# Four-layer graph kernel: the last rows of layer 0 in two groups, gate weights between root and rows, x transfers moved

## The chip, the cores and the metric

The kernel runs on one core of a Trainium2 chip. Times are device microseconds of one execution. TensorE (PE) multiplies, VectorE (DVE), ScalarE (ACT) and GpSimd (POOL) work elementwise, and SyncE (SP) issues DMAs. Each engine runs its own list of instructions in order; they meet at semaphores.

## The reference

There are 4096 nodes with 64 features and a sparse 0/1 matrix adj of 4096 x 4096. Four graph layers follow one another, each with a residual and a layer norm. Cut to what matters:

```python
# layer 0: the last 100 neighbours of each row, weights halved with each step back
rank = cumsum(mask, axis=1); deg = rank[:, -1:]
w = mask * where(pos > 0, 0.5 ** (k - pos), 0)
x = layernorm(x + w @ (x @ W0) + b0)
# layer 1: two gated steps (GRU), each over the whole matrix
m = adj @ (x @ W); gi = m @ wih.T + bih; gh = x @ whh.T + bhh
r, z = sigmoid(...), sigmoid(...); n = tanh(i_n + r * h_n)
h = relu((1 - z) * n + z * x)          # and once more with other weights
x = layernorm(x + h2)
# layers 2 and 3: a normalized product, a mean over neighbours
x = layernorm(x + (dinv * (adj + I) * dinv) @ x @ W2)
x = layernorm(x + concat([x, adj @ x / (deg + 1)]) @ W3.T)
```

## The kernel before, in words

The program numbers its five passes over the matrix 0 to 4: pass 0 is the first layer (called layer 0 in the code and here), 1 and 2 are the gated steps, 3 and 4 the last two layers. The matrix stays in SBUF as fp8 (adjT). Nodes come in 32 tiles of 128 (index jb), or 8 groups g of 512. A pass computes for each group g the product of all 32 tiles of the rows S (a high and a low f16 piece of the scaled x, 128 columns together) with 512 columns of adjT: product(layer, g, first, last), L1083, issues the matmuls of tiles first to last. combine(layer, g), L911, applies the small weights to the finished group.

Layer 0 goes in four quarters q of 1024 nodes (Q = 4, B = 4 tiles in a group). Each quarter ends in rows0 (L562) and norm (L516) on VectorE: sums, means, squares and variances, each as two instructions (both_halves, L499), then a wait for GpSimd. There root (L302) raises the variances to the power -1/2; it waits for var_ready and signals rstd_ready. Then VectorE writes the normalized rows xrow, and split_rows0 (L581) makes of them the two pieces of S[1] and adds 2 to s_ready, one for each group. For the last quarter that is L807, L808 and the last root, L337.

The products of the gated pass on tiles 0 to 23 are placed in layer 0, in slots on TensorE (BETWEEN, L1026), and at the head of layer1 (L1132). What needs tiles 24 to 31 waits for the last quarter: product waits for s_ready to reach 8 + jb / 4 + 1. Between them stand gate_sums (L1109), which multiplies weight pairs in PSUM and turns the degrees, and open_gates (L1122), which waits for the four signals of gate_const and for the degrees (deg_step), and clears the gate banks. Behind open_gates ScalarE writes the biases (seed, L422), and ScalarE and VectorE form m of the first group (take_y, hi_of_m, m_lo): the m path. combine(1, 0) waits for that and for the x transfer below.

gate_weights (L711) on VectorE forms the gates' constants: two zero fills, wx16 and part of wl16 out of the loaded weights w_h (gate_const 1), the biases (2, 3), and wm16 and the rest of wl16 out of gate_sums' result (4). degrees (L811) follows.

SP's queue: it loads biases and w_gates (L262) and the degree rows when layer 0 has ended, then transposes each group of S[1] into x16 by DMA (loop at L274). The upper half of x16 holds the loaded weights until they are used, so the fifth transpose waits for gate_const 4. x_high (L266) copies the high piece of a group beside m (mx16, three buffers, x_beside). The first three stand behind the eighth transpose. The order on each engine is the order in which the code is written; nothing reorders it.

Of the kernel before, what the change touches and what calls it, by code (L numbers as in the profile page):

```python
# [21 lines left out]
N, D = 4096, 64  # L22
P = 128
# [40 lines left out]
def build(nc, a):  # L64
    with ExitStack() as ctx:
# [182 lines left out]
        def _(sp):  # L248
# [25 lines left out]
            for layer in TURNS:  # L274
                for g in range(G):
                    sp.wait_ge(s_ready, layer * G + g + 1)
                    if layer == 1 and g == G // 2:
                        sp.wait_ge(gate_const, 4)
                    if layer > 1:
                        sp.wait_ge(combined, min(layer, 3) * G - G + g + 1)  # L280
                    sp.dma_start_transpose(x16[:, g * GC:(g + 1) * GC].rearrange("p (b r) -> p b r", b=B),  # L281
                                           S[layer % 2][:, g * B:(g + 1) * B, :].rearrange("p b d -> p (b d)"))\
                        .then_inc(xT_in[g], 16)
                    if layer == 2:
                        x_high(1 + (g + 3) // G, (g + 3) % G)
                if layer == 1:
                    sp.wait_ge(masked_ready, Q * NM * B)
                    x_high(1, 0)
                    x_high(1, 1)
                    x_high(1, 2)  # L290
                if layer == 2:
                    for g in range(3, G):
                        x_high(2, g)
# [7 lines left out]
        def _(pool):  # L301
            def root(n, blocks):  # L302

                pool.wait_ge(var_ready, n + 1)
                nc.gpsimd.tensor_tensor(rstd[:, 0:blocks], stat[:, 2, 0:blocks], mhalf[:, 0:blocks], ALU.pow)\  # L305
                    .then_inc(rstd_ready, 1)
# [30 lines left out]
            root(Q - 1, 2 * B)  # L337
# [6 lines left out]
            for layer in (2, 3, 4):  # L344
                for g, (_, nb) in enumerate(UNITS[layer]):
                    n = Q + (layer - 2) * G + g
# [140 lines left out]
        def _(dve):  # L487
# [11 lines left out]
            def both_halves(step, signal=None):  # L499


                for h in range(2):
# [3 lines left out]
                    if h == 1 and signal is not None:  # L506
                        ins.then_inc(signal, 1)
                    else:
                        did(ins)
                        last[h] = steps[0]  # L510
# [5 lines left out]
            def norm(n, z, zc, sq, dst, ready, meanwhile=None):  # L516
# [11 lines left out]
                                                              ALU.mult, ALU.add), var_ready)  # L528
# [33 lines left out]
            def rows0(q, out=True):  # L562
# [8 lines left out]
                norm(q, wide[0], wide[1], wide[2], pair if out else None, rows0_ready)  # L571
# [139 lines left out]
            def gate_weights():  # L711
# [7 lines left out]
                                               op0=ALU.mult, op1=ALU.subtract).then_inc(gate_const, 1)  # L719
                dve.wait_ge(biases_in, 16)  # L720
# [86 lines left out]
            rows0(Q - 1)  # L807
            split_rows0(Q - 1)  # L808
            gate_weights()

# [33 lines left out]
            for layer in range(1, LAYERS):  # L844
# [7 lines left out]
                for g, (b0, nb) in enumerate(UNITS[layer]):  # L852
# [49 lines left out]
                    norm(Q + (layer - 2) * G + g, z[:, 0:nb, :], zc[:, 0:nb, :], sq[:, 0:nb, :],  # L902
# [7 lines left out]
        def _(pe):  # L910
# [198 lines left out]
            def gate_sums():  # L1109
# [8 lines left out]
                pe.wait_ge(rows0_ready, Q)  # L1118
# [3 lines left out]
            def open_gates():  # L1122

                pe.wait_ge(rows0_ready, Q)
# [7 lines left out]
            def layer1():  # L1132
# [3 lines left out]
                product(1, 3, 0, 24)  # L1136
                gate_sums()
                product(1, 0, 24, 32)
                product(1, 1, 24, 31)
                open_gates()  # L1140
                product(1, 1, 31, 32)
                product(1, 2, 24, 32)
                product(1, 3, 24, 32)
                product(1, 4, 0, 9)
                combine(1, 0)
                product(1, 4, 9, 23)
                combine(1, 1)
                product(1, 4, 23, 32)
                product(1, 5, 0, 5)
                combine(1, 2)  # L1150
                product(1, 5, 5, 20)
                combine(1, 3)
                product(1, 5, 20, 32)
                product(1, 6, 0, 4)
                combine(1, 4)
                product(1, 6, 4, 20)
                combine(1, 5)
                product(1, 6, 20, 32)
# [171 lines left out]
```

## Time and profile before

| | before |
|---|---|
| median of 3 runs | 430.13 us (429.86 to 430.8) |
| profiled execution | 430.51 us |
| its span | 428.7 us |
| PE busy | 404.7 us, 94% |
| DVE / ACT / POOL busy | 295.4 / 215.1 / 116.8 us |
| mean granted clock of TensorE | 0.99 |

The span is the time between the first and last instruction of the profiled execution; the execution itself is longer by what lies around it. Matmuls overlap, so a row of products is busy for longer than the pitch of its instructions times their number by the tail of its last one. In a timeline the bracket behind a row is the idle time of that engine before it, and what ended it.

### The profile page before, as it was taken

To read this page: it belongs to the slowest core of one execution; us is meant where nothing else is said; L and a number is where in the kernel's file an instruction comes from. 1 tells how busy PE (TensorE), PEld (TensorE's weight loads), DVE (VectorE), ACT (ScalarE), POOL (GpSimd) and SP (SyncE) were. 2 spreads that over 40 slices of the span, in tenths; PEclk is the share of its full clock that TensorE was granted. 3 is DMA by queue.
4 is the path that set the end of the run, shared out by engine and by line. 5 is a ranking of instruction groups with operands and counts; after the bars stand their busy time and mean duration, and the time that the engine had idled before them with its cause. 6 is when DMAs were issued, how large, how long until landed. Compare 5 with 4: busy or idle time off the path is not lost.

```text
span 428.7 us, 6431 instructions
## 1 busy us (share of the span) xinstructions
PE 404.7 (94%) x2243; PEld 191.2 (45%) x2258; DVE 295.4 (69%) x862; ACT 215.1 (50%) x345; POOL 116.8 (27%) x154
## 2 busy tenths in 40 slices
PE   5878989999999999998999999999999999999991
PEld 2332433434344444444555555555554444445480
DVE  3377968867976787473964566776949566477773
ACT  2566788688868877506864554635222121212100
POOL 8213223231420100015231304234325434311111
PEclk9998999999999999999999999999999999999997
DMA  8999999999999994173011110000000101100000
GB/s 144 108 115 106 107 107 108 107 108 107 109 107 107 107 108 44 44 95 67 20 42 33 38 32 6 8 7 2 0 2 13 27 12 26 26 14 26 25 26 13
DMA packets 26241, 24.68 MB, mean 58 GB/s; under 512 B 14776, under 2 KB 17624, under 8 KB 26208
## 3 DMA queue, kind: packets, MB, share of 16 engines
q0 software_dynamic: 9360, 16.78, 39.1%
q1 hardware_dynamic: 16704, 7.41, 8.0%
q8 instruction: 18, 0.29, 0.3%
q10 hardware_dynamic: 144, 0.07, 0.1%
q14 instruction: 15, 0.12, 0.1%
HBM read 69.32 MB, written 1.06 MB: 164 GB/s over the span
## 4 chain that ended last, share of the span: by engine, by line
PE 80%; DMA 7%; DVE 4%; POOL 2%; issue 2%; ACT 1%; SPq 1%; POOLq 0%; DVEq 0%; ACTq 0%
PE Y L1099 45%; PE both L1008 15%; DMA adjT<-in_adjT 6%; PE both L987 3%; PE Y L987 3%; PE both L1015 3%; PE both L999 2%; PE Y L999 2%; PE both L959 2%; SPq L281 1%; PE both L955 1%; PE both L957 1%; POOL rstd L305 1%; POOL adjT L333 1%; DMA work<-x 1%
## 5 line engine op out<-in xcount | busy, mean ns | idle before, releaser
L1099 PE MATMUL Y<-adjT,S 128*128 128x512 fp8e4 (+1 forms) x1056 | 231.0, 373 | 0.8 <-DVE S L587 0.8
L1099 PEld LDWEIGHTS Y<-adjT,S 128*128 128x128 f16 x1056 | 101.8, 98 | 109.0 <-DVE S L587 0.9
L417 ACT ACTIVATE wgt<-both,consts 128x512 int16<-128x512 f32 x160 | 106.9, 687 | 33.6 <-PE both L1008 29.9
L305 POOL TENSOR_TENSOR rstd<-stat,mhalf 128x4 f32<-128x4 f32 (+2 forms) x29 | 35.1, 1212 | 149.1 <-DVE stat L527 149.1
L1008 PE MATMUL both<-adjT,tri 128*128 128x512 fp8e4 x160 | 61.3, 384 | 2.9 <-DMA adjT<-in_adjT 2.7
L1008 PE MATMUL both<-adjT,fix 128*128 128x512 fp8e4 x152 | 58.4, 384 | 2.3 <-ACT wgt L417 1.1
L333 POOL DMA_DIRECT2D adjT<-in_adjT x63 | 36.9, 593 | 78.8 <-DMA adjT<-in_adjT 78.8
L547 DVE SCALAR_TENSOR_TENSOR work<-Y,yT 64x512 f32<-64x512 f32 x30 | 20.8, 695 | 47.6 <-ACT yT L376 47.4
L376 ACT ACTIVATE yT<-Y 64x512 f32<-64x512 f32 x30 | 17.6, 587 | 65.2 <-PE Y L1099 41.6
L320 POOL TENSOR_TENSOR S<-work,S 128x256 f16<-128x256 f32 x24 | 18.8, 785 | 48.0 <-ACT S L401 27.4
L387 ACT ACTIVATE work<-work 64x512 f16<-64x512 f32 x30 | 18.8, 627 | 26.1 <-DVE work L547 24.6
L1008 PEld LDWEIGHTS both<-adjT,fix 128*128 128x128 bf16 x152 | 14.8, 97 | 37.6 <-ACT wgt L417 22.8
L987 PE MATMUL both<-wgt,S 128*128 128x512 bf16 x77 | 29.4, 381 | 0.3 <-ACT wgt L417 0.3
L987 PE MATMUL Y<-wgt,S 128*128 128x512 bf16 x72 | 27.3, 379 | 0.0
L614 DVE TENSOR_SCALAR work<-adjT 128x3072 int16<-128x3072 fp8e4 x12 | 21.1, 1756 | 7.6 <-PE both L999 7.6
L637 DVE TENSOR_TENSOR work<-work 128x1024 uint16<-128x1024 int16 x36 | 24.6, 684 | 0.9 <-ACT work L414 0.3
L626 DVE TENSOR_TENSOR work<-work 128x1024 int16<-128x1024 int16 x36 | 24.6, 682 | 0.0
L414 ACT ACTIVATE work<-both,consts 128x512 int16<-128x512 f32 x24 | 16.0, 688 | 15.8 <-PE both L1015 15.7
L433 ACT ACTIVATE both<-biases 128x1024 f32<-128x1024 f32 x16 | 16.1, 1011 | 15.0 <-PE both L1128 15.0
L553 DVE TENSOR_TENSOR work<-work 64x512 f16<-64x512 f32 x30 | 20.6, 687 | 3.6 <-ACT work L387 2.8
L1008 PEld LDWEIGHTS both<-adjT,tri 128*128 128x128 bf16 x160 | 15.7, 98 | 13.2 <-issue 5.1
L603 DVE TENSOR_TENSOR x<-adjT 128x1024 uint16<-128x1024 uint16 x12 | 8.2, 686 | 17.5 <-DMA adjT<-in_adjT 14.5
(129 smaller groups left out, 477.6 us busy)
## 6 DMA issues: line engine op xcount, KB each, us to landing
adjT<-in_adjT POOLq DMA_DIRECT2D x63, 256.0 KB, 39.0
work<-x SPq DMA_DIRECT2D x16, 64.0 KB, 2.0
out_rows<-xrow SPq DMA_DIRECT2D x7, 128.0 KB, 1.9
xrow<-in_xrow SPq DMA_DIRECT2D x1, 640.0 KB, 7.2
x<-in_w_gates SPq DMA_DIRECT2D x1, 512.0 KB, 5.8
biases<-in_biases SPq DMA_DIRECT2D x1, 384.0 KB, 4.2
x<-S SPq DMA_TRANSPOSE x24, 2.4
xrow<-in_xrow SPq DMA_DIRECT2D x1, 256.0 KB, 3.6
```

The source lines that it names most:

```text
L305: nc.gpsimd.tensor_tensor(rstd[:, 0:blocks], stat[:, 2, 0:blocks], mhalf[:, 0:blocks], ALU.pow)\
L320: nc.gpsimd.tensor_tensor(s[:, :, D:2 * D], ts[:, :, :], s[:, :, 0:D], ALU.subtract).then_inc(s_ready, 1)
L333: pool.dma_start(adjT[:, q, 2 * jp:2 * jp + 2, :], a["adjT"][q, jp]).then_inc(load[i % NLOAD], 16)
L417: nc.scalar.activation(wgt[:, c, tiles % 2, :], V[c][:, :], ACT.Relu, bias=tile_bias[sums]).then_inc(w_ready[c], 1)
L547: nc.vector.scalar_tensor_tensor(out=m[D:P, e % 2, :], in0=bank(layer, g)[D:P, :], scalar=1.0 / SCALE, in1=yT[D:P, e % 2, :], op0=ALU.mult ...
L553: nc.vector.tensor_tensor(m16[0:D, e % 2, :], m[D:P, e % 2, :], m16[D:P, e % 2, :], ALU.subtract)\
L614: nc.vector.tensor_scalar(wq[:, 1:B, :], adjT[:, q, quad * B + 1:(quad + 1) * B, :], -float(STEP), None, ALU.mult)\
L626: nc.vector.tensor_tensor(wq[:, k, :], wq[:, k, :], seen_now, ALU.bitwise_and).then_inc(masked_ready, 1)
L637: nc.vector.tensor_tensor(out.bitcast(U16), seen_now, wq[:, k, :], ALU.add).then_inc(seen_step, 1)
L987: mm = nc.tensor.matmul(own[c], S[0][:, jb, :], wgt[:, c, TILES.index(jb) % 2, :].bitcast(BF16), start=first, stop=(jb == 0), skip_group_c ...
L1008: return nc.tensor.matmul(V[c][:, :], (tri, fix)[which][:, :], adj_tile(q, at, c), start=start, stop=(which == 0 and s == NS - 1), skip_gr ...
L1099: mm = nc.tensor.matmul(bank(layer, g)[:, 0:nb * P], S[layer % 2][:, jb, :], cols[:, jb, :], start=(jb == 0), stop=(jb == JB - 1), skip_gr ...
```

## The change

The last 1024 rows are normalized by two roots of four columns in place of one of eight. In norm both halves of the variances now signal var_ready (each=True), and a new function last_rows writes xrow and S[1] for groups 6 and 7 apart, with one signal for each. Later roots and norms count one higher. gate_weights is cut in two: the part that works on w_h alone stands ahead of last_rows, and the rest (gate_products) behind it. On TensorE four products of tiles 24 to 27 stand ahead of gate_sums, open_gates comes after ten more products in place of fifteen, and one product of pass 1 goes from before combine(1, 0) to behind combine(1, 5). On SP the first three x_high stand ahead of the fifth transpose.

```diff
--- before.py
+++ after.py
@@ -275,6 +275,9 @@
                 for g in range(G):
                     sp.wait_ge(s_ready, layer * G + g + 1)
                     if layer == 1 and g == G // 2:
+                        sp.wait_ge(masked_ready, Q * NM * B)
+                        for first in range(3):
+                            x_high(1, first)
                         sp.wait_ge(gate_const, 4)
                     if layer > 1:
                         sp.wait_ge(combined, min(layer, 3) * G - G + g + 1)
@@ -283,11 +286,6 @@
                         .then_inc(xT_in[g], 16)
                     if layer == 2:
                         x_high(1 + (g + 3) // G, (g + 3) % G)
-                if layer == 1:
-                    sp.wait_ge(masked_ready, Q * NM * B)
-                    x_high(1, 0)
-                    x_high(1, 1)
-                    x_high(1, 2)
                 if layer == 2:
                     for g in range(3, G):
                         x_high(2, g)
@@ -299,10 +297,10 @@
 
         @block.gpsimd
         def _(pool):
-            def root(n, blocks):
+            def root(n, blocks, first=0):
 
                 pool.wait_ge(var_ready, n + 1)
-                nc.gpsimd.tensor_tensor(rstd[:, 0:blocks], stat[:, 2, 0:blocks], mhalf[:, 0:blocks], ALU.pow)\
+                nc.gpsimd.tensor_tensor(rstd[:, first:first + blocks], stat[:, 2, first:first + blocks], mhalf[:, 0:blocks], ALU.pow)\
                     .then_inc(rstd_ready, 1)
 
             def split_rows(layer, g):
@@ -334,7 +332,8 @@
                     if q >= 2 and n == 5:
                         root(q - 2, 2 * B)
             root(Q - 2, 2 * B)
-            root(Q - 1, 2 * B)
+            root(Q - 1, B)
+            root(Q, B, B)
 
             pool.wait_ge(deg_step, 1)
             nc.gpsimd.tensor_tensor(dinv[:, :], deg1[:, :], mhalf[:, :], ALU.pow).then_inc(dinv_pow, 1)
@@ -343,7 +342,7 @@
             pool.wait_ge(dinv_ready, 2)
             for layer in (2, 3, 4):
                 for g, (_, nb) in enumerate(UNITS[layer]):
-                    n = Q + (layer - 2) * G + g
+                    n = Q + 1 + (layer - 2) * G + g
                     root(n, nb)
                     if layer == 2 and g < G - 1:
 
@@ -496,14 +495,14 @@
 
                 dve.wait_ge(chain, steps[0])
 
-            def both_halves(step, signal=None):
+            def both_halves(step, signal=None, each=False):
 
 
                 for h in range(2):
                     if last[h] > 0:
                         dve.wait_ge(chain, last[h])
                     ins = step(h)
-                    if h == 1 and signal is not None:
+                    if (h == 1 or each) and signal is not None:
                         ins.then_inc(signal, 1)
                     else:
                         did(ins)
@@ -513,7 +512,7 @@
 
                 return [slice(h * blocks // 2, (h + 1) * blocks // 2) for h in range(2)]
 
-            def norm(n, z, zc, sq, dst, ready, meanwhile=None):
+            def norm(n, z, zc, sq, dst, ready, meanwhile=None, each=False):
 
 
                 H = halves(z.shape[1])
@@ -525,7 +524,7 @@
                 both_halves(lambda h: nc.vector.tensor_tensor(sq[:, H[h], :], zc[:, H[h], :], zc[:, H[h], :], ALU.mult))
                 both_halves(lambda h: nc.vector.tensor_reduce(stat[:, 1, H[h]], sq[:, H[h], :], AX, ALU.add))
                 both_halves(lambda h: nc.vector.tensor_scalar(stat[:, 2, H[h]], stat[:, 1, H[h]], 1.0 / D, EPS,
-                                                              ALU.mult, ALU.add), var_ready)
+                                                              ALU.mult, ALU.add), var_ready, each)
                 if dst is None:
                     return
                 if meanwhile is not None:
@@ -559,7 +558,7 @@
                 nc.vector.tensor_tensor(xrow[:, 2 * q * B:(2 * q + 2) * B, :], wide[1],
                                         rstd[:, :, None].to_broadcast([P, 2 * B, D]), ALU.mult).then_inc(rows0_ready, 1)
 
-            def rows0(q, out=True):
+            def rows0(q, out=True, each=False):
 
                 pair = xrow[:, 2 * q * B:(2 * q + 2) * B, :]
                 if q == 0:
@@ -568,7 +567,21 @@
                 both_halves(lambda h: nc.vector.scalar_tensor_tensor(
                     out=wide[0][:, h * B:(h + 1) * B, :], in0=gates[0][:, 2 + h, :].rearrange("p (b d) -> p b d", d=D),
                     scalar=1.0 / (Y0_SCALE * SCALE), in1=pair[:, h * B:(h + 1) * B, :], op0=ALU.mult, op1=ALU.add))
-                norm(q, wide[0], wide[1], wide[2], pair if out else None, rows0_ready)
+                norm(q, wide[0], wide[1], wide[2], pair if out else None, rows0_ready, each=each)
+
+            def last_rows():
+
+                for h in range(2):
+                    g = G - 2 + h
+                    blk, part = slice(g * B, (g + 1) * B), slice(h * B, (h + 1) * B)
+                    dve.wait_ge(rstd_ready, Q + h)
+                    nc.vector.tensor_tensor(xrow[:, blk, :], wide[1][:, part, :],
+                                            rstd[:, part, None].to_broadcast([P, B, D]), ALU.mult).then_inc(rows0_ready, 1)
+                    dve.wait_ge(rows0_ready, Q + h)
+                    did(nc.vector.tensor_scalar(S[1][:, blk, 0:D], xrow[:, blk, :], SCALE, None, ALU.mult))
+                    after()
+                    nc.vector.scalar_tensor_tensor(out=S[1][:, blk, D:2 * D], in0=xrow[:, blk, :], scalar=SCALE,
+                                                   in1=S[1][:, blk, 0:D], op0=ALU.mult, op1=ALU.subtract).then_inc(s_ready, 1)
 
             def pick_degree(q, c):
 
@@ -717,6 +730,8 @@
                 after()
                 nc.vector.scalar_tensor_tensor(out=wl16[0:D, :, 0:3 * D], in0=w_h[0:D, :, :], scalar=GATE / SCALE, in1=wx16[0:D, :, :],
                                                op0=ALU.mult, op1=ALU.subtract).then_inc(gate_const, 1)
+            def gate_products():
+
                 dve.wait_ge(biases_in, 16)
                 nc.vector.tensor_tensor(gbias[:, :, D:3 * D], gbias[:, :, D:3 * D], brz, ALU.add).then_inc(gate_const, 1)
                 dve.wait_ge(gate_const, 2)
@@ -804,9 +819,10 @@
             take_y(0, 6)
             take_y(0, 7)
 
-            rows0(Q - 1)
-            split_rows0(Q - 1)
+            rows0(Q - 1, False, True)
             gate_weights()
+            last_rows()
+            gate_products()
 
             def degrees():
 
@@ -899,7 +915,7 @@
                         both_halves(lambda h: nc.vector.tensor_tensor(z[:, H[h], :], t1[:, H[h], :], t2[:, H[h], :], ALU.add))
                     if layer == 2 and g >= 1:
                         dve.wait_ge(rows_ready, G + g)
-                    norm(Q + (layer - 2) * G + g, z[:, 0:nb, :], zc[:, 0:nb, :], sq[:, 0:nb, :],
+                    norm(Q + 1 + (layer - 2) * G + g, z[:, 0:nb, :], zc[:, 0:nb, :], sq[:, 0:nb, :],
                          None if layer == 2 and g < G - 1 else xrow[:, blk, :], rows_ready,
                          messages)
                     if layer == 4 and in_halves(4, g + 1):
@@ -1115,13 +1131,13 @@
                     mm.then_inc(gate_prod, 1)
                 pe.wait_ge(deg_in, 16)
                 pe.wait_ge(unit_ready, 1)
-                pe.wait_ge(rows0_ready, Q)
+                pe.wait_ge(rows0_ready, Q + 1)
                 nc.tensor.matmul(gates[0][:, 2, 0:JB], deg_mat[:, :], identity[0:JB, 0:JB], start=True, stop=True)\
                     .then_inc(deg_turned, 1)
 
             def open_gates():
 
-                pe.wait_ge(rows0_ready, Q)
+                pe.wait_ge(rows0_ready, Q + 1)
                 pe.wait_ge(gate_const, 4)
                 pe.wait_ge(deg_step, 1)
                 for half in range(2):
@@ -1134,28 +1150,29 @@
                 combine(0, 6)
                 combine(0, 7)
                 product(1, 3, 0, 24)
+                product(1, 0, 24, 28)
                 gate_sums()
-                product(1, 0, 24, 32)
-                product(1, 1, 24, 31)
+                product(1, 0, 28, 32)
+                product(1, 1, 24, 30)
                 open_gates()
-                product(1, 1, 31, 32)
+                product(1, 1, 30, 32)
                 product(1, 2, 24, 32)
                 product(1, 3, 24, 32)
-                product(1, 4, 0, 9)
+                product(1, 4, 0, 8)
                 combine(1, 0)
-                product(1, 4, 9, 23)
+                product(1, 4, 8, 22)
                 combine(1, 1)
-                product(1, 4, 23, 32)
-                product(1, 5, 0, 5)
+                product(1, 4, 22, 32)
+                product(1, 5, 0, 4)
...
```

VectorE between the statistics of the last quarter and the degrees; wl and wx are the gate weights, S the pieces. Before:

```order
L535 TENSOR_TENSOR xrow<-hrow,rstd 128x512 [waits rstd_ready]
L585 TENSOR_SCALAR S<-xrow 128x8x64 [waits rows0_ready]
L587 SCALAR_TENSOR_TENSOR S<-xrow,S 128x8x64 [waits chain]
L714 MEMSET wl 64x2x32 [waits gate_in]
L715 MEMSET wl 64x2x32
L716 TENSOR_SCALAR wx<-x 128x384
L718 SCALAR_TENSOR_TENSOR wl<-x,wx 64x2x192 [waits chain]
L721 TENSOR_TENSOR biases<-biases 128x2x128 [waits biases_in]
L723 TENSOR_SCALAR biases<-biases 128x512 [waits gate_const]
L726 TENSOR_SCALAR wm<-both 128x384 [waits gate_prod]
L728 SCALAR_TENSOR_TENSOR wl<-both,wm 64x2x192 [waits chain]
L814 TENSOR_SCALAR deg<-both 128x32 [waits deg_turned,gate_const]
```

and now, where gate_prod's waiter follows behind the last row shown:

```order
L727 MEMSET wl 64x2x32 [waits gate_in]
L728 MEMSET wl 64x2x32
L729 TENSOR_SCALAR wx<-x 128x384
L731 SCALAR_TENSOR_TENSOR wl<-x,wx 64x2x192 [waits chain]
L578 TENSOR_TENSOR xrow<-hrow,rstd 128x256 [waits rstd_ready]
L581 TENSOR_SCALAR S<-xrow 128x4x64 [waits rows0_ready]
L583 SCALAR_TENSOR_TENSOR S<-xrow,S 128x4x64 [waits chain]
L578 TENSOR_TENSOR xrow<-hrow,rstd 128x256 [waits rstd_ready]
L581 TENSOR_SCALAR S<-xrow 128x4x64 [waits rows0_ready]
L583 SCALAR_TENSOR_TENSOR S<-xrow,S 128x4x64 [waits chain]
L736 TENSOR_TENSOR biases<-biases 128x2x128 [waits biases_in]
L738 TENSOR_SCALAR biases<-biases 128x512 [waits gate_const]
```

Four instructions of gate_weights have moved ahead of the wait for rstd_ready, and three row instructions of 512 columns have become six of 256.

TensorE from gate_sums (the 128x192 matmuls on x) to open_gates (ones, cutw). Before:

```order
L1114 MATMUL both<-x 128x192 [waits y0_out1,gate_in]
L1114 MATMUL both<-x 128x192
L1119 MATMUL both<-unit,deg_mat 128x32 [waits rows0_ready,unit_ready,deg_in]
L1099 MATMUL Y<-adjT,S 128x512 [waits s_ready]
L1099 MATMUL Y<-adjT,S 128x512 x3
L1099 MATMUL Y<-adjT,S 128x512 [waits s_ready]
L1099 MATMUL Y<-adjT,S 128x512 x3
L1099 MATMUL Y<-adjT,S 128x512 [waits s_ready]
L1099 MATMUL Y<-adjT,S 128x512 x3
L1099 MATMUL Y<-adjT,S 128x512 [waits s_ready]
L1099 MATMUL Y<-adjT,S 128x512 x2
L1128 MATMUL both<-ones,cutw 128x512 [waits deg_step,gate_const,rows0_ready]
```

and now:

```order
L1115 MATMUL Y<-adjT,S 128x512 [waits s_ready]
L1115 MATMUL Y<-adjT,S 128x512 x3
L1130 MATMUL both<-x 128x192 [waits y0_out1,gate_in]
L1130 MATMUL both<-x 128x192
L1135 MATMUL both<-unit,deg_mat 128x32 [waits rows0_ready,unit_ready,deg_in]
L1115 MATMUL Y<-adjT,S 128x512 [waits s_ready]
L1115 MATMUL Y<-adjT,S 128x512 x3
L1115 MATMUL Y<-adjT,S 128x512 [waits s_ready]
L1115 MATMUL Y<-adjT,S 128x512 x3
L1115 MATMUL Y<-adjT,S 128x512 [waits s_ready]
L1115 MATMUL Y<-adjT,S 128x512
L1144 MATMUL both<-ones,cutw 128x512 [waits deg_step,gate_const,rows0_ready]
```

Four products with their wait for s_ready stand ahead of gate_sums, and ten in place of fifteen between it and open_gates.

SP's queue from the first transpose of the rows (x<-S) to the x transfers (work<-x). Before:

```order
L281 DMA_TRANSPOSE x<-S 128x4x128 [waits s_ready] x4
L281 DMA_TRANSPOSE x<-S 128x4x128 [waits gate_const,s_ready]
L281 DMA_TRANSPOSE x<-S 128x4x128 [waits s_ready] x3
L272 DMA work<-x 64x512 [waits xT_in0,masked_ready]
L272 DMA work<-x 64x512 [waits xT_in1]
L272 DMA work<-x 64x512 [waits xT_in2]
```

and now:

```order
L284 DMA_TRANSPOSE x<-S 128x4x128 [waits s_ready] x4
L272 DMA work<-x 64x512 [waits xT_in0,masked_ready,s_ready]
L272 DMA work<-x 64x512 [waits xT_in1]
L272 DMA work<-x 64x512 [waits xT_in2]
L284 DMA_TRANSPOSE x<-S 128x4x128 [waits gate_const]
L284 DMA_TRANSPOSE x<-S 128x4x128 [waits s_ready] x3
```

The three transfers stand ahead of the transpose that waits for gate_const.

## Rows read from the trace of the kernel before

**Rows 1.** The page's part 4, shares of the span by engine.

```profile
PE 80%; DMA 7%; DVE 4%; POOL 2%; issue 2%; ACT 1%; SPq 1%; POOLq 0%; DVEq 0%; ACTq 0%
```

**Rows 2.** The chain that ended last: start us, us, what.

```profile
186.05 1.65 POOL rstd L305
...
188.98 0.69 DVE S L587
...
192.19 0.57 DVE wl L728
...
198.04 1.98 DMA work<-x
...
231.16 6.91 PE Y L1099 x32
```

**Rows 3.** Timeline, 178 to 206 us, TensorE: start us, us, engine, line.

```profile
182.17 5.34 PE L1099 MATMUL Y<-adjT,S 128*128 128x512 fp8e4 x24
...
187.44 0.92 PE L1114 MATMUL both<-x 64*128 64x192 f32 x4
...
188.56 0.38 PE L1119 MATMUL both<-unit,deg_mat 32*128 32x32 f32 x2 [0.20 <-DVE xrow L535]
...
189.73 3.41 PE L1099 MATMUL Y<-adjT,S 128*128 128x512 fp8e4 x15 [0.79 <-DVE S L587]
...
193.56 5.77 PE L1099 MATMUL Y<-adjT,S 128*128 128x512 fp8e4 x26
...
200.27 0.24 PE L955 MATMUL both<-wx,x 128*128 128x192 f16 x1 [0.94 <-DMA work<-x]
```

**Rows 4.** Waits of TensorE from 200 us to the end: total, times, longest.

```profile
PE both L955 <- DMA work<-x: 1.4, 2, 0.9
```

**Rows 5.** Timeline, 178 to 206 us, VectorE.

```profile
185.69 0.28 DVE L527 TENSOR_SCALAR stat<-stat 128x4 f32<-128x4 f32 x2
...
189.63 0.11 DVE L714 MEMSET wl<- 64x64 uint32 x1
...
190.82 0.41 DVE L721 TENSOR_TENSOR biases<-biases 128x256 f32<-128x256 f32 x1
...
191.61 0.55 DVE L726 TENSOR_SCALAR wm<-both 128x384 f16<-128x384 f32 x1
...
192.79 0.19 DVE L814 TENSOR_SCALAR deg<-both 128x32 f32<-128x32 f32 x1
```

**Rows 6.** Timeline, VectorE, 256-column instructions, 0 to 36 us and 322 to 326 us.

```profile
29.47 0.28 DVE L669 TENSOR_SCALAR S<-xrow 128x256 f16<-128x256 f32 x1
29.78 0.43 DVE L671 SCALAR_TENSOR_TENSOR S<-xrow,S 128x256 f16<-128x256 f32 x1
...
324.73 0.43 DVE L535 TENSOR_TENSOR xrow<-work,rstd 128x256 f32<-128x256 f32 x1 [0.18 <-POOL rstd L305]
```

**Rows 7.** Timeline, VectorE and GpSimd around two later roots.

```profile
323.14 0.69 DVE L553 TENSOR_TENSOR work<-work 64x512 f16<-64x512 f32 x1
323.19 1.51 POOL L305 TENSOR_TENSOR rstd<-stat,mhalf 128x4 f32<-128x4 f32 x1 [8.26 <-DVE stat L527]
...
379.11 0.69 DVE L547 SCALAR_TENSOR_TENSOR work<-Y,yT 64x512 f32<-64x512 f32 x1
379.16 1.01 POOL L305 TENSOR_TENSOR rstd<-stat,mhalf 128x4 f32<-128x4 f32 x1 [8.29 <-DVE stat L527]
```

**Rows 8.** Timeline, 178 to 206 us, the end of the m path.

```profile
197.76 0.69 DVE L553 TENSOR_TENSOR work<-work 64x512 f16<-64x512 f32 x1 [0.69 <-ACT work L387]
```

**Rows 9.** DMA issues and landing: w_gates; transposes issued 180 to 184 us.

```profile
179.19 0.43 SPq L262 DMA_DIRECT2D x<-in_w_gates  x1
...
x<-in_w_gates SPq DMA_DIRECT2D x1, 512.0 KB, 5.8
...
DMA to landing us min/median/max: 5.2/6.0/6.9
```

**Rows 10.** Busy time by stretch: us, busy by engine, granted clock.

```profile
186.80:189.90 3.10, 2.10 (x11) 1.12 (x10) 1.97 (x5) 0.00 (x0) 0.89 (x1) 1.00 0.41 81
```

More of the change, by code:

```diff
@@ L1136, in layer1 @@
                 product(1, 3, 0, 24)
+                product(1, 0, 24, 28)
                 gate_sums()
-                product(1, 0, 24, 32)
-                product(1, 1, 24, 31)
+                product(1, 0, 28, 32)
+                product(1, 1, 24, 30)
                 open_gates()
-                product(1, 1, 31, 32)
+                product(1, 1, 30, 32)
                 product(1, 2, 24, 32)
                 product(1, 3, 24, 32)
-                product(1, 4, 0, 9)
+                product(1, 4, 0, 8)
                 combine(1, 0)
-                product(1, 4, 9, 23)
+                product(1, 4, 8, 22)
                 combine(1, 1)
-                product(1, 4, 23, 32)
-                product(1, 5, 0, 5)
+                product(1, 4, 22, 32)
+                product(1, 5, 0, 4)
                 combine(1, 2)
-                product(1, 5, 5, 20)
+                product(1, 5, 4, 19)
                 combine(1, 3)
-                product(1, 5, 20, 32)
-                product(1, 6, 0, 4)
+                product(1, 5, 19, 32)
+                product(1, 6, 0, 3)
                 combine(1, 4)
-                product(1, 6, 4, 20)
+                product(1, 6, 3, 19)
                 combine(1, 5)
-                product(1, 6, 20, 32)
+                product(1, 6, 19, 32)
                 product(1, 7, 0, 17)
```

## The prediction

> **What bounds the kernel now.** I read four views in this order. First the page's shares of the chain that ended last: TensorE carries 80% of it [rows 1], so time is won only where TensorE stands still or where a chain feeds it late. Second, the chain itself between layer 0 and layer 1: it leaves TensorE at the last root on GpSimd (186.05, 1.65 us), goes on over the rows on VectorE (the second of the two S instructions starts at 188.98), the gate constants (last one at 192.19) and the DMA queue, and ends in the transfer that starts at 198.04 and takes 1.98 us [rows 2]. Third, TensorE's timeline over the same stretch, where the holes are [rows 3]. Fourth, the waits of TensorE from 200 us to the end: on the gate sums' DMA it waits 1.4 us in two places, 0.94 of it in the hole just named, the rest once later [rows 4]. So after combine(1, 0) TensorE is fed almost without a break, each later step hangs on a step before it, and what combine(1, 0) gains or loses the end gains or loses.
>
> The holes add up as follows. A product matmul in an unbroken row costs 6.91 / 32 = 0.216 us [rows 2]. From 182.17 to the start of combine(1, 0) at 200.27 are 18.10 us. In them stand 24 + 15 + 26 = 65 products (14.04), gate_sums with the turned degrees (187.44 to 188.94, less the 0.20 idle shown: 1.30) and two matmuls of open_gates (0.43): 15.77 of work [rows 3]. The other 2.33 us are waits: 0.09 before gate_sums, 0.20 for the rows, 0.79 for the two pieces S, about 0.16 before open_gates (189.73 + 15 x 0.216 = 192.97, while the 26 products begin at 193.56, so the pair at 193.13), and 200.27 - (193.56 + 5.62) = 1.09 for the x transfer.
>
> **The change part by part.**
>
> *The x transfers.* They stood behind the fifth transpose, which waits for gate_const, and three more of about 1.3 us each on SP's queue. Now they stand ahead of it. What they need is there early: the first transpose is issued at 180.13 and lands after at most 6.9 us, at 187.0 [rows 9]. Three issues and 1.98 us for landing [rows 2] bring the last one home by about 191, eight microseconds before use. Queued behind them are only transposes 5 to 8; these start no earlier than gate_const anyway, and their data is used four combines later. So the DMA part of the 1.09 goes, and what is late next is the m path: ScalarE and VectorE need from open_gates to the end of the instruction at 197.76, that is 198.45 [rows 8]. That is 0.7 us before TensorE would be there at 199.18, so it makes no wait.
>
> *gate_weights between the root and the rows.* Its first four instructions take 190.82 - 189.63 = 1.19 us [rows 5]. VectorE is free at 185.69 + 0.28 = 185.97 and idles until the root is there, so they run until 187.16. They now lie beside the root and cost only what sticks out past it.
>
> *Two roots in place of one.* The first of the two statistics instructions ends at 185.83 and the root began 0.08 after its input: 185.91. A root of 4 columns takes 1.01 us where nothing disturbs it and 1.51 in layer 3 [rows 7]; this case shows neither beside these memsets. With 1.01 it ends at 186.92, before VectorE is free at 187.16, and costs nothing; I take this value, since at its start VectorE runs a memset of a tenth of a microsecond, not the two-source instruction of 0.69 us that stands beside the slow roots. The far end is that it is held up until VectorE is through with gate_weights, then about 0.9 us late.
>
> *Rows in halves.* For 256 columns: 0.43 and a gap of 0.04 for the normalized rows, 0.31 from the start of the first S instruction to the second, 0.43 for that: 1.21 us [rows 6]. First S pieces at 187.16 + 1.21 = 188.37; TensorE starts 0.06 behind (189.73 after 188.98 + 0.69), at 188.43. The second root runs to about 188.0, hidden by the first rows, and the second pieces are ready at 188.37 + 1.21 = 189.58.
>
> *TensorE's new order.* The 24 products end at 187.35 as before. Four products on the first pieces now stand ahead of gate_sums, so TensorE waits 1.08 us in one piece there, where gate_sums used to fill 1.3 us. That is a price of the new order. Then: 188.43 + 4 x 0.216 = 189.29; 0.09 + 1.30 gives 190.68; the second pieces (189.58) are there; ten products, 192.84. open_gates waits for gate_const 4 and for the degrees. gate_products follow the rows: 189.58 + 0.79 = 190.37, when gate_sums (189.29 + 0.09 + 0.92 = 190.30) has just come; then 192.79 - 191.61 = 1.18 gives 191.55, and about 0.2 for the degrees [rows 3, 5]. That is 1.1 us ahead of 192.84, no wait. The pair ends at 193.27, 26 products bring combine(1, 0) to 198.89. open_gates comes 193.13 - 192.84 = 0.29 earlier, so the m path ends at 198.16: still no wait.
>
> *The sum.* 200.27 - 198.89 = 1.38 us earlier. One product of the 65 is moved from before combine(1, 0) to behind combine(1, 5), where TensorE doesn't wait: 0.22 is given back. Net 1.16 us, or in waits: 2.33 go, 1.08 + 0.09 come. The profiled execution would be 430.51 - 1.16 = 429.35. It stands 0.38 above the median of 430.13, which I move by the same amount: 428.97 us.
>
> *A rule against it.* The rows show that the root beside VectorE's m_lo, which reads two tensors in SBUF, takes 1.51, and beside the instruction at 379.11, one of whose sources is in PSUM, 1.01 [rows 7]. The Trainium skill, GPSIMD Engine Reference, section "Key points", says that GpSimd shares its SBUF interfaces with VectorE and contends with instructions in a 2-port mode or with two SBUF inputs. These rows agree. By that rule the root would meet the wx and wl instructions, both of that kind, which VectorE did not run beside it before.
>
> **The rivals.**
>
> 1. *The root is slowed beside gate_weights.* For it: 1.51 in seven of the eight roots of layer 3. Against: an instruction that starts when the root is under way seems to cost nothing. Price: the root ends at 187.42, the rows start at 187.45 in place of 187.16, 0.29 us: a gain of 0.87, 429.3 us. At the far end of the bounds above the gain is 1.16 - 0.9 = 0.3, 429.9.
>
> 2. *The gain is given back at open_gates or combine(1, 0).* VectorE now has six row instructions in place of three, and both gate_const and the degrees lie behind them. If roots and rows stretch by more than 1.1 us, open_gates waits for the degrees, one for one, and with it the m path. Then the gain is 0 to 0.4, some 429.9 us. For it: the second root is exposed to three instructions, two of them with two SBUF sources. Against: two slacks of 1.1 us in a row.
>
> 3. *Slower: w_gates isn't there.* VectorE now waits for it at 185.97 with the rows queued behind, where before it was first needed at 187.44. The load is issued at 179.19 and lands after 5.8 us, at 184.99 [rows 9], 0.98 ahead. Each microsecond past 185.97 delays the rows by as much; from 187.1 on the whole gain is gone, and from 188.0 on the kernel is slower by over 0.2%. For it: the transposes issued behind that load took 5.2 to 6.9 us to land, so the engines were crowded. Against: one measured landing, and the same queue order now. At 188.5 it would be 431.5 us.
>
> A lower clock after the unbroken wait of 1.08 us I rate as nothing: TensorE worked 2.10 of 3.10 us around the old holes at a granted clock of 1.00, that is 2.4 GHz [rows 10].
>
> **How the numbers follow.** Forecast as worked out (gain 0.95 to 1.35): 0.58. Rival 1: 0.20. Rival 2: 0.14. Rival 3: 0.08. A difference of 0.2% is 0.86 us, about what a measurement of this kernel can tell from none. The forecast lies above it but for 0.02, rival 1 half on each side: faster 0.56 + 0.10, and a little of rival 2, 0.67. Slower is most of rival 3: 0.07. Same is the rest, 0.26. Range: from a gain of 1.5 (the small gaps vanish as well, and the measurement's own spread) to one of 0.2, which leaves out rival 3 and part of rival 2: 428.6 to 429.9 us.
>
> **What would show it.** In the new trace: combine(1, 0) starts with no DMA wait, about 1.4 us earlier; one wait of about 1.1 us ahead of the four products, released by the first S piece, and none at gate_sums, the other S piece or open_gates; the first root 1.0 (or 1.5, rival 1); the four gate_weights instructions beside it; the later wait for the x transfer at combine(1, 3) unchanged at about 0.45. I am wrong if open_gates or combine(1, 0) shows a wait of over 0.3 us, or if the memsets wait for a DMA.

## The result, and the profile after

| | before | changed |
|---|---|---|
| median of 20 runs each | 430.1 us | 429.29 us |
| ratio, 95% interval | | 0.9979 (0.9972 to 0.9987) |
| profiled execution, its span | 430.51, 428.7 us | 429.43, 427.6 us |
| VectorE instructions in the trace | 862 | 865 |

By the ratio the change gains 0.90 us (0.21% of 430.1); the two medians are 0.81 apart. The forecast was 428.97, a gain of 1.16: right in direction and chain, a quarter of a microsecond too large by the ratio. The ratio's interval lies wholly below 1, but it holds the 0.2% that the prediction took as what can just be told from none. In the page of the changed kernel each engine is busy for the same share within 1%, and TensorE has 83% of the chain that ended last, where it had 80%. Such averages say little of a gain of 0.2%, so the answer is in the stretch of [rows 3]. Its TensorE timeline now, columns as there:

```profile
182.09 5.34 PE L1115 MATMUL Y<-adjT,S 128*128 128x512 fp8e4 x24
...
188.29 1.04 PE L1115 MATMUL Y<-adjT,S 128*128 128x512 fp8e4 x4 [0.85 <-DVE S L583]
...
189.26 0.91 PE L1130 MATMUL both<-x 64*128 64x192 f32 x4
...
190.10 0.40 PE L1135 MATMUL both<-unit,deg_mat 32*128 32x32 f32 x2
...
190.44 2.33 PE L1115 MATMUL Y<-adjT,S 128*128 128x512 fp8e4 x10
...
193.04 5.78 PE L1115 MATMUL Y<-adjT,S 128*128 128x512 fp8e4 x26
...
198.65 0.25 PE L971 MATMUL both<-wx,x 128*128 128x192 f16 x1
```

From the 24 products to combine(1, 0) it was 18.10 us in [rows 3]; it is 198.65 - 182.09 = 16.56. One wait is left, ahead of the four products, and the transfer no longer holds up combine(1, 0). VectorE, GpSimd and SP beside it, where [rows 5, 2, 9] stood:

```profile
185.62 0.28 DVE L526 TENSOR_SCALAR stat<-stat 128x4 f32<-128x4 f32 x2
185.84 0.11 DVE L727 MEMSET wl<- 64x64 uint32 x1
185.85 2.47 POOL L303 TENSOR_TENSOR rstd<-stat,mhalf 128x4 f32<-128x4 f32 x2 [36.04 <-DVE stat L526]
...
186.56 0.55 DVE L731 SCALAR_TENSOR_TENSOR wl<-x,wx 64x384 f16<-64x384 f32 x1
186.62 1.82 SPq L272 DMA_DIRECT2D work<-x  x3
187.04 0.41 DVE L578 TENSOR_TENSOR xrow<-hrow,rstd 128x256 f32<-128x256 f32 x1
...
187.81 0.43 DVE L583 SCALAR_TENSOR_TENSOR S<-xrow,S 128x256 f16<-128x256 f32 x1
...
188.35 0.43 DVE L578 TENSOR_TENSOR xrow<-hrow,rstd 128x256 f32<-128x256 f32 x1
...
191.45 5.13 SPq L284 DMA_TRANSPOSE x<-S  x4
191.45 0.19 DVE L830 TENSOR_SCALAR deg<-both 128x32 f32<-128x32 f32 x1
```

The four gate_weights instructions fill the time of the first root, the first group's rows follow without a gap, and the transfers leave SP at 186.62, 11.4 us earlier, ahead of the transposes that wait for gate_const.

All that TensorE waits for over 0.15 us from 180 us to the end (total, times, longest):

```profile
PE Y L1115 <- DVE S L583: 0.9, 1, 0.9
PE both L971 <- DMA work<-x: 0.4, 1, 0.4
PE both L982 <- ACT yT L378: 0.4, 1, 0.4
```

The later wait of 0.4 for a transfer is that of [rows 4]. Up to combine(4, 6), in the last pass, the gain holds. Then 0.3 us go, in the last 16 us, called the tail here. The end of the kernel before, which stood in no row so far:

```profile
407.15 0.40 PE L963 MATMUL both<-w_o,work 128*128 128x64 f16 x8
407.36 0.49 DVE L891 SCALAR_TENSOR_TENSOR work<-both,xrow 128x128 f32<-128x128 f32 x2 [0.83 <-PE both L928]
...
407.76 0.48 DVE L895 TENSOR_TENSOR work<-both,rdeg 128x128 f32<-128x128 f32 x2
...
423.12 0.29 DVE L535 TENSOR_TENSOR xrow<-work,rstd 128x128 f32<-128x128 f32 x1 [0.81 <-POOL rstd L305]
```

and of the changed one:

```profile
405.74 0.40 PE L979 MATMUL both<-w_o,work 128*128 128x64 f16 x8
405.94 0.49 DVE L907 SCALAR_TENSOR_TENSOR work<-both,xrow 128x128 f32<-128x128 f32 x2 [0.84 <-PE both L944]
...
406.68 0.49 DVE L911 TENSOR_TENSOR work<-both,rdeg 128x128 f32<-128x128 f32 x2 [0.26 <-DVE work L907]
...
422.03 0.29 DVE L534 TENSOR_TENSOR xrow<-work,rstd 128x128 f32<-128x128 f32 x1 [0.81 <-POOL rstd L303]
```

TensorE is 1.41 us earlier, the first VectorE instruction 1.42, the next only 1.08: it starts 0.74 behind its predecessor where it was 0.40. The bracket shows 0.26 of that as idle time, although its releaser, the row above, had ended at 406.43. From there the chain that ended last runs over VectorE and GpSimd alone in both traces, so the last rows are 1.09 earlier.

### The profile page after: what moved, and what is told of

Its sections match the earlier page's. It is cut to its first block, busy times and chain, and to the rows that moved or that the text cites. A ratio compares the mean times of both kernels' runs of the same rounds, so it can differ in the third digit from the quotient of the medians.

```text
span 427.6 us, 6433 instructions
## 1 busy us (share of the span) xinstructions
PE 404.6 (95%) x2243; PEld 191.3 (45%) x2258; DVE 295.6 (69%) x865; ACT 215.1 (50%) x345; POOL 117.9 (28%) x155
## 4 chain that ended last, share of the span: by engine, by line
PE 83%; DMA 7%; DVE 3%; POOL 2%; issue 2%; ACT 1%; SPq 0%; POOLq 0%; ACTq 0%
PE Y L1115 47%; PE both L1024 15%; DMA adjT<-in_adjT 6%; PE both L1003 3%; PE Y L1003 3%; PE both L1031 3%; PE both L1015 2%; PE Y L1015 2%; PE both L975 2%; PE both L971 1%; PE both L973 1%; POOL adjT L331 1%; PE both L966 1%; PE both L979 1%; POOL rstd L303 1%
```

## The experiments

Executions begin this stretch up to 2.4 us apart, so the traces are best compared from the start of the 24 products. Each entry is the difference of two starts in the same trace: to the first matmul of combine(1, 0), to the first w_o matmul of combine(4, 6), and to VectorE's last write of xrow (the last rows); then combine(4, 6) to the last rows, the tail. In the three traces of the changed kernel itself these differences agree within 0.04 us. A gain in us that stands beside a ratio is worked out from that ratio.

| kernel | combine(1, 0) | combine(4, 6) | last rows | tail | ratio to before (interval) |
|---|---|---|---|---|---|
| before | 18.10 | 224.98 | 240.95 | 15.97 | |
| changed | 16.56 | 223.65 | 239.94 | 16.29 | 0.9979 (0.9972, 0.9987) |
| x_alone | 16.99 | 223.88 | 239.85 | 15.97 | 0.9975 (0.9966, 0.9984) |
| x_back | 16.84 | 223.96 | 240.29 | 16.33 | 0.9977 (0.9968, 0.9986) |
| gates_split | 15.75 | 222.84 | 239.15 | 16.31 | 0.9963 (0.9949, 0.9977) |
| after_again | 16.56 | 223.66 | 239.98 | 16.32 | 0.9981 (0.9972, 0.9989) |
| one_root | 16.85 | 223.74 | 239.69 | 15.95 | 0.9971 (0.9961, 0.9981) |
| late_rows | 17.34 | 224.44 | 240.38 | 15.94 | 0.9994 (0.9980, 1.0008) |
| pad4 | 16.56 | 223.65 | 239.60 | 15.95 | 0.9967 (0.9954, 0.9980) |
| split_pad4 | 15.75 | 222.84 | 238.78 | 15.94 | 0.9952 (0.9939, 0.9966) |
| pad1 | 16.56 | 223.74 | 239.70 | 15.96 | one time, 429.45 us |
| pad2 | 16.56 | 223.66 | 239.63 | 15.97 | one time, 428.88 us |
| after_third | 16.56 | 223.65 | 239.96 | 16.31 | 0.9975 (0.9966, 0.9984) |
| pad4_again | 16.55 | 223.65 | 239.61 | 15.96 | 0.9964 (0.9952, 0.9977) |

**x_alone.** One part of the change, put into the kernel before.

```diff
...
                     if layer == 1 and g == G // 2:
+                        sp.wait_ge(masked_ready, Q * NM * B)
+                        for first in range(3):
+                            x_high(1, first)
                         sp.wait_ge(gate_const, 4)
...
-                if layer == 1:
-                    sp.wait_ge(masked_ready, Q * NM * B)
-                    x_high(1, 0)
-                    x_high(1, 1)
-                    x_high(1, 2)
...
```

> The kernel before with one edit: the first three x transfers stand ahead of the fifth transpose. My theory: the wait of 1.09 us at combine(1, 0) goes whole, because TensorE would be there at 199.18 and the m path is through at 198.45; combine(1, 0) starts at about 199.2 and the kernel gains 1.0 to 1.1 us, more than the whole change measured. Rival (the two groups of rows carry the gain and the transfer is only one of several things that end at about 200): combine(1, 0) stays near 200 and the gain is under 0.4 us.

Measured: 0.9975, that is 1.08 us, and combine(1, 0) 1.11 us earlier in its stretch. Its row, without a wait, after 26 products that start at 192.85:

```profile
192.85 5.77 PE L1097 MATMUL Y<-adjT,S 128*128 128x512 fp8e4 x26
...
198.46 0.25 PE L953 MATMUL both<-wx,x 128*128 128x192 f16 x1
```

My theory held: four moved lines on SP bring as much as the whole change. The medians of both on one chip were 429.17 for this and 429.23 for the changed kernel run again (after_again, below). The traces tell them apart: up to combine(4, 6) the whole change is 0.23 us ahead of this part, and at the last rows it is 0.09 behind, because of its longer tail.

**x_back.** The changed kernel without that part.

```diff
...
-                        sp.wait_ge(masked_ready, Q * NM * B)
-                        for first in range(3):
-                            x_high(1, first)
...
+                if layer == 1:
+                    sp.wait_ge(masked_ready, Q * NM * B)
+                    x_high(1, 0)
+                    x_high(1, 1)
+                    x_high(1, 2)
...
```

> The changed kernel with the three x transfers put back behind the eighth transpose. My theory: the old chain from gate_const over four transposes to the transfer took 200.27 - 192.83 = 7.44 us; gate_const comes at 191.4 now, so combine(1, 0) starts at about 198.9 in place of 198.65, and 0.2 to 0.3 us of the gain are lost, no more: either part alone takes most of the gain. Rival (the parts add up): 1.0 us or more is lost and the kernel is as slow as before.

Measured: combine(1, 0) 0.28 us later than in the changed kernel. SP's queue and the combine:

```profile
191.31 5.12 SPq L281 DMA_TRANSPOSE x<-S  x4
196.52 1.82 SPq L272 DMA_DIRECT2D work<-x  x3
...
198.75 0.24 PE L973 MATMUL both<-wx,x 128*128 128x192 f16 x1
```

191.31 + 7.44 is 198.75 to the digit. Two edits open the same wait, by 1.1 and by 1.3 us, and together by 1.5: their gains overlap. The ratios can't tell 0.28 us (0.9977 against 0.9979 and 0.9981); the traces do.

**gates_split.** gate_sums' two weight products stand ahead of the four products again.

```diff
...
                     mm.then_inc(gate_prod, 1)
+
+            def turn_degrees():
+
                 pe.wait_ge(deg_in, 16)
...
                 product(1, 3, 0, 24)
+                gate_sums()
                 product(1, 0, 24, 28)
-                gate_sums()
+                turn_degrees()
                 product(1, 0, 28, 32)
...
```

> The changed kernel with gate_sums' weight products put ahead of the four early products again, and only the turned degrees behind them. My theory: the wait of 0.94 us that the new order made ahead of the four products is filled by the 0.92 us of weight products, combine(1, 0) starts at about 197.8 in place of 198.65, and the kernel gains another 0.7 to 0.9 us. Rival (open_gates waits for gate_const and the degrees, which VectorE has at 191.7 at the earliest, or the m path holds combine(1, 0)): a gain under 0.3 us.

Measured: combine(1, 0) another 0.81 us earlier, the ratio 0.9963. TensorE no longer waits in this stretch:

```profile
189.13 0.91 PE L1130 MATMUL both<-x 64*128 64x192 f32 x4
...
190.06 1.04 PE L1115 MATMUL Y<-adjT,S 128*128 128x512 fp8e4 x4
...
191.38 2.33 PE L1115 MATMUL Y<-adjT,S 128*128 128x512 fp8e4 x10
```

So the change's order of TensorE cost 0.81 us, nearly the whole of the wait of 0.85 that stood ahead of the four products. (This trace runs later as a whole, by 1.8 us at the 24 products; its granted clock was 0.83 over the first 20 us, against 1.00 in the changed kernel's trace.)

**one_root.** Everything but the two groups, with TensorE's order of before.

```diff
...
-            root(Q - 1, B)
-            root(Q, B, B)
+            root(Q - 1, 2 * B)
...
             gate_weights()
-            last_rows()
+            rows0_out(Q - 1)
+            split_rows0(Q - 1)
             gate_products()
...
```

> The changed kernel with one root of eight columns and whole rows as before, gate_weights still between root and rows, the x transfers still moved, and TensorE's order of the kernel before. What is tested: whether two roots and the four early products bring anything. My theory: almost nothing, since the new order pays with a wait of 0.94 us for what gate_sums filled; here the second pieces come at 189.6 as before, gate_const 1.2 us after earlier, combine(1, 0) about 1.35 us earlier than before (0.95 if the root is slowed to 2.07 us), and the gain is 1.0 to 1.3 us, no less than the whole change's 0.9. Rival (the halves carry a good part): a gain at or below that of the x transfers alone, 1.07 us, with combine(1, 0) at 1.1 or less.

Measured: 0.9971, 1.25 us. The root was not slowed beside gate_weights:

```profile
186.26 1.64 POOL L303 TENSOR_TENSOR rstd<-stat,mhalf 128x8 f32<-128x8 f32 x1 [36.17 <-DVE stat L525]
...
187.93 0.69 DVE L557 TENSOR_TENSOR xrow<-hrow,rstd 128x512 f32<-128x512 f32 x1 [0.53 <-POOL rstd L303]
...
189.93 3.41 PE L1115 MATMUL Y<-adjT,S 128*128 128x512 fp8e4 x15 [0.79 <-DVE S L599]
```

It still has the old waits of 0.20 and 0.79. At combine(1, 0) it is 0.29 us behind the changed kernel, but 0.22 of that is the product that the change put behind combine(1, 5). To combine(4, 6), with that product in both, it is 0.09 behind: so much do two groups and the four early products bring together. At the last rows it is 0.25 ahead, because its tail is the short one.

**late_rows.** wx16 computed three times in a row ahead of last_rows.

```diff
...
                 did(nc.vector.tensor_scalar(wx16[:, :, :], w_h, GATE / SCALE, None, ALU.mult))
                 after()
+                did(nc.vector.tensor_scalar(wx16[:, :, :], w_h, GATE / SCALE, None, ALU.mult))
+                after()
+                did(nc.vector.tensor_scalar(wx16[:, :, :], w_h, GATE / SCALE, None, ALU.mult))
+                after()
...
```

> The changed kernel with the wx instruction (0.37 us, 0.40 from one to the next) issued three times in a row, the last result the same. The rows begin 0.8 us later. My theory: the first pieces lie on the path one for one, and so combine(1, 0) and the end come 0.8 us later, and the gain of the change is gone (within 0.2 us of the kernel before). Rival (the slack of 1 us behind the rows covers it): under 0.3 us lost.

Measured: combine(1, 0) 0.78 us later than in the changed kernel, the wait ahead of the four products 1.64 in place of 0.85, the ratio 0.9994, 0.26 us ahead of the kernel before and not to be told from it. So the instructions between root and rows are free only as far as the first root reaches; past it they count one for one up to combine(4, 6). At the last rows this trace is only 0.44 behind the changed kernel, since it has the short tail.

```profile
189.27 1.04 PE L1119 MATMUL Y<-adjT,S 128*128 128x512 fp8e4 x4 [1.64 <-DVE S L583]
```

**after_again, after_third, and the padded ones.** These are about the tail. after_again and after_third are the changed kernel without an edit. The others put one, two or four memsets, each of one column of an unused tile, at the head of VectorE's list. The edit with one:

```diff
...
+        spare = sb("spare", [P, 64])
...
+            nc.vector.memset(spare[:, 0:1], 0.0)
             nc.vector.memset(cutw[:, :], -float(CUT) / P).then_inc(const_ready, 1)
...
```

> The changed kernel once more. combine(1, 0) came 1.62 us earlier in its trace and combine(4, 6) 1.41, but the last rows only 1.08: in the tail VectorE began one instruction 0.34 us late. My theory: this belongs to one execution; here the gap of 0.24 us ahead of the rdeg product on VectorE is gone and the last rows come about 1.4 us earlier than before. Rival (the shifted program makes it, every time): the same gap at the same place, and a median gain of about 0.9 us against 1.2.

Here my theory fell: the same gap of 0.26 us stood ahead of the same instruction, and the gain was near the rival's 0.9 us (0.82, from 0.9981). The traces with the changed kernel's VectorE list, 865 instructions, have it, x_back and gates_split among them: five of five with after_third. before, x_alone and one_root (862) do not.

> The changed kernel with four memsets of one column to an unused tile at the start of VectorE's list, where VectorE waits for a load. The gap of 0.24 us ahead of the rdeg product stood in all four traces of programs with the new VectorE list and in neither with the old one. Theory: it goes with the position of the instruction in VectorE's list; moved by four it disappears from the last 20 us and the kernel gains 0.3 us on the change. Rival (it comes from the phase between TensorE and VectorE, not from the position): the gap stays where it is and the time as well.

> The weight products of gate_sums ahead of the four early products, together with the four memsets of pad4. By the position theory it gains 0.3 us on gates_split, 2.0 us or more on the kernel before, and is the fastest; by the rival as fast as gates_split, 1.6 us ahead of before.

> The changed kernel with one memset to an unused tile at the start of VectorE's list. Position theory: the gap of 0.26 us moves up by one instruction and stands between the two instructions that scale the own rows (the second starts 0.7 us after the first in place of 0.4), still on the path, and the last rows come as late as in the changed kernel. Phase theory: it stays ahead of the rdeg product.

> The same with two memsets. Position theory: the gap stands ahead of the first of the two, where VectorE waits 0.84 us for TensorE, and is not seen; the tail is as short as with four. Phase theory: it stays ahead of the rdeg product.

> The changed kernel, to be compared on one chip with the same one padded by four memsets: 0.9 us ahead of before, the gap of 0.26 us again ahead of the rdeg product.

> The changed kernel with four memsets at the start of VectorE's list. Position theory: 0.3 us ahead of the changed kernel on the same chip, 1.1 to 1.4 us ahead of before, as TensorE's start of combine(4, 6) was 1.41 us early in the first trace of the changed kernel. Rival: the 1.4 us of the first run came from that chip's disturbances, and both are equal.

Measured with four memsets, VectorE at the place of the gap:

```profile
405.80 0.49 DVE L912 SCALAR_TENSOR_TENSOR work<-both,xrow 128x128 f32<-128x128 f32 x2 [0.84 <-PE both L949]
406.21 0.48 DVE L916 TENSOR_TENSOR work<-both,rdeg 128x128 f32<-128x128 f32 x2
```

The distance is 0.41 again, the tail 15.95 and 15.96 in the two runs, in place of 16.29. On one chip the medians were 429.16 for the changed kernel and 428.71 padded. Against before on that chip the padded kernel gained 1.55 us (0.9964) and the changed one 1.08 (0.9975), each a little above what I had expected. TensorE's stretches are the same to 0.01 us with and without those four, so a phase between TensorE and VectorE is ruled out; what counts is VectorE's list. But the position theory in its strict form missed as well: with one memset the gap should have moved up by one instruction and stayed on the path, and it is not there; the tail is 15.96. Nor does late_rows show it, with two instructions more than the changed kernel. So at this place the gap stands in lists of 865 instructions, and not in those of 862, 866, 867 and 869.

One memset did not do away with such gaps, though. pad1 has two of the same 0.26 us that the changed kernel has not, at 278.25 and here:

```profile
364.49 0.97 DVE L905 TENSOR_TENSOR work<-work,xrow 128x128 f32<-128x128 f32 x2 [0.26 <-DVE work L901]
```

They cost little where they lie: TensorE shows no new wait of over 0.15 us, and combine(4, 6) comes 0.09 us later in its stretch than in the changed kernel.

The traces also hold a candidate for the cause. Part 3 of the page counts small transfers on queues of the kind instruction. In each of the five traces with the gap in the tail, one of 8 KB on q14 starts 0.66 to 0.69 us after the late instruction (407.36 after 406.68 in the changed kernel), and in pad1 one starts 0.67 us after the instruction at 364.49 and one 1.0 us after that at 278.25. It moves with the list: it starts 1.6 us after combine(4, 6) with 865 instructions and 0.3 us ahead of it with 866 and 867, where VectorE waits for TensorE. In the changed kernel the queue view from 406.7 to 408.5 us has this one transfer alone:

```profile
q14 instruction: 1, 0.01, 1.8%
```

Against it as the whole cause: with 862 instructions such a transfer starts 1.7 us after combine(4, 6), and no instruction beside it is late. So that the gaps go with the loading of VectorE's instructions is likely, and not shown; the mechanism stays open.

split_pad4, the order of gates_split with the four memsets, has the lowest median and ratio: 428.20 us, 0.9952 of before, 2.1 us. Its last rows are 0.37 us ahead of gates_split's in their stretch.

## Why the prediction was right, and where it was off

*The x transfers.* Right. Hidden from 186.62 on; the wait of 0.94 [rows 3] gone, and the m path, named as next, not reached: its last instruction ended 0.7 us or more before combine(1, 0) in every run.

*gate_weights beside the root.* Right, and a little better: VectorE resumed at 185.84, before its second statistics instruction had ended at 185.90. I had counted from that end.

*Two roots.* The first took 1.01 us, the value taken. Rival 1's mechanism came true for the second root alone, which began 0.27 us after the wl instruction had started:

```profile
186.83 1.49 POOL L303 TENSOR_TENSOR rstd<-stat,mhalf 128x4 f32<-128x4 f32 x1
```

The sum had it hidden behind the first rows; for VectorE it was not quite. It ended at 188.32 in place of about 188.0, and the second rows began at 188.35, 0.54 us after the S instruction ahead of them; in late_rows, where the second root took 1.00, that distance is 0.34. So it held VectorE up by 0.2 us. TensorE felt nothing: the second pieces were ready at 189.56, 0.9 us before they were used, and open_gates did not wait.

*Rows in halves.* From 187.04 to 188.24, 1.20 us; 1.21 was predicted.

*TensorE's order.* The wait ahead of the four products is 188.29 - (182.09 + 5.18) = 1.02 us by the pitch, 1.08 predicted. gate_sums and the turned degrees took 190.44 - 189.26 = 1.18, not 1.30: without a wait around them each row begins before the last one has ended (190.10 against 189.26 + 0.91, 190.44 against 190.10 + 0.40). combine(1, 0) came 1.54 us earlier in its stretch, 1.38 predicted; at combine(4, 6), with the moved product paid back, 1.33 against 1.16.

*The sum.* The step that failed is "what combine(1, 0) gains or loses the end gains or loses". It holds for TensorE to 0.01 us over 200 us, once the moved product is paid back, but the last 16 us belong to VectorE and GpSimd, and there the changed program gave back 0.32. 1.33 - 0.32 = 1.01 is left from the 24 products on; the profiled execution is 1.08 shorter, since it also began the stretch 0.08 earlier. The ratios of three sets give 0.82 to 1.08. That the forecast came as near as a quarter of a microsecond is in part luck: the stretch gained 0.17 more than predicted, and the tail, which I had left out, took 0.32.

*Rivals 2 and 3.* Neither happened. The degrees were there at 191.64, 1.0 us before open_gates. w_gates made no wait at 185.84.

*A slip in the reading.* The 1.4 us of [rows 4] were called waits for the gate sums' DMA. The row names work<-x: they are waits for the x transfers, as the rest of the prediction takes them.

What I did not ask is what each part was worth alone. The x transfers alone bring 1.08 by the ratio, the whole 0.82 to 1.08.

## What to carry to other kernels

If two edits each remove what holds the same instruction, their gains don't add; look for the cheapest one first. When a wait is moved to the front, ask what used to fill it: here 0.92 us of independent products had been moved behind it, and putting them back was worth 0.8 us more, nearly as much as the whole change had gained. The end of a kernel has a bound of its own; read the last chain in both traces before taking a gain in the middle as a gain of the whole.

## What the runs showed of the hardware

*A root took half a microsecond longer when an instruction with two SBUF sources was running on VectorE as it began.* The Trainium skill, GPSIMD Engine Reference, section "Key points", names two SBUF inputs and 2-port modes. For the former the traces agree: the second root of the changed kernel, begun at 186.83 while the wl instruction ran on two SBUF tensors, took 1.49, and in the trace of before the five roots of layer 3 that had m_lo alone beside them took 1.51. In late_rows the same root began beside wx, which has one SBUF source (384 columns in 0.36 us, against 0.55 for wl's 384):

```profile
187.02 1.00 POOL L303 TENSOR_TENSOR rstd<-stat,mhalf 128x4 f32<-128x4 f32 x1
...
187.14 0.36 DVE L733 TENSOR_SCALAR wx<-x 128x384 f16<-128x384 f32 x1
```

It took 1.00. So for this one-source form no contention shows; whether it is the 2-port mode that the Trainium skill names there, no run here shows. What runs when the root begins seems to decide: the wl instruction started when the root was 0.52 us old in late_rows and 0.58 in one_root, and the roots kept their 1.00 and 1.64. Two things stay open. The slow root of the changed kernel also met the normalized rows, two SBUF sources, at an age of 0.21 us, and no run puts those there without wl. And the first root of late_rows took 1.11 in place of 1.01, and no instruction beside it had two sources.

*A gap of about 0.3 us on VectorE depends on the program's list.* At one instruction of the tail it stood in five of five traces of one list and in none of nine of the other lists, with TensorE's stretches equal. Three more instructions at 186 us cost 0.32 us at 406 us; one memset at the start, in idle time, took that away and left two such gaps where they cost little. The cause is open.
